# Ninety-six semaphore increments on SP behind each broadcast of lanes, in the layer 1 visits of a graph network

## What is computed

```
h = (x @ W).reshape(n, 4, 64)
h_l = (a_l * h).sum(-1);  h_r = (a_r * h).sum(-1)
e = h_l[row] + h_r[col];  e = where(e > 0, e, 0.2 * e)
ex = exp(e - segment_max(e, row)[row])
att = ex / (segment_sum(ex, row)[row] + 1e-16)
out = segment_sum(att[:, :, None] * h[col], row)
```

## Time and profile before

| | us |
|---|---|
| median of 3 runs | 4150.6 |
| lowest and highest of them | 4141.25, 4151.45 |
| the profiled execution | 4167.99 |
| its span, from the first to the last instruction | 4166.3 |
| the first and the last broadcast of lanes start at | 2048.0, 3372.1 |

### The profile page before, as it was taken

One profiled execution on the slowest core, in us unless ns is written; L12 is line 12 of the kernel. 1 busy time (PEld: TensorE's weight loads), 2 busy tenths in 40 slices (PEclk: granted clock), 3 DMA queues, 4 the chain that ended last, 5 costly groups with the idle time before them and its releaser, 6 DMA issues. The chain is left out here.

```text
span 4166.3 us, 48622 instructions
## 1 busy us (share of the span) xinstructions
PE 2771.2 (67%) x12850; PEld 2189.0 (53%) x12850; DVE 2489.0 (60%) x5847; ACT 1566.9 (38%) x5077; POOL 2220.9 (53%) x2162
## 2 busy tenths in 40 slices
PE   5466776567677754824666676666667665699983
PEld 4233344355555543713555465555555545599972
DVE  5345998677777786434545555555555567544438
ACT  6663000067787831113422232233233223333334
POOL 0366777766666602555256666666666641265530
PEclk9678888788898965967867767677776675799985
DMA  5232333323333313632234444444444464122234
GB/s 146 86 88 83 89 87 89 88 85 90 90 93 91 95 57 91 152 76 71 78 89 114 109 114 113 109 115 109 113 113 112 111 112 150 62 72 70 71 96 143
DMA packets 220767, 408.50 MB, mean 98 GB/s; under 512 B 51598, under 2 KB 134545, under 8 KB 220371
## 3 DMA queue, kind: packets, MB, share of 16 engines
q0 software_dynamic: 102192, 279.12, 25.2%
q1 hardware_dynamic: 118308, 126.27, 10.2%
HBM read 342.96 MB, written 62.28 MB: 97 GB/s over the span
## 5 line engine op out<-in xcount | busy, mean ns | idle before, releaser
L534 POOL DMA_INDIRECT arena<-h_table,arena x1712 | 1751.6, 1023 | 1016.0 <-issue 482.5
L548 DVE TENSOR_TENSOR arena<-arena,ps 128x260 f32 (+1 forms) x1712 | 719.6, 420 | 905.0 <-remote 407.0
L2199 PE MATMUL ps<-arena 128*128 128x260 f32 x1760 | 667.1, 538 | 415.9 <-DVE arena L548 282.6
L2199 PEld LDWEIGHTS ps<-arena 128*128 128x128 f32 x1760 | 441.5, 268 | 591.3 <-issue 457.0
L1216 PE MATMUL ps<-arena 128*128 128x256 f32 x1664 | 556.7, 451 | 252.5 <-DVE arena L548 133.1
L1216 PEld LDWEIGHTS ps<-arena 128*128 128x128 f32 x1664 | 328.1, 222 | 410.2 <-issue 238.2
L717 ACT ACTIVATE arena<-arena 128x112 f16<-128x112 f16 x1568 | 446.5, 375 | 88.1 <-DVE arena L983 77.6
L2066 ACT ACTIVATE ps<-arena 128x32 f32<-128x32 f32 x110 | 22.1, 201 | 953.8 <-DVE arena L2122 784.6
L884 DVE TENSOR_SCALAR arena<-arena 128x128 f32<-128x128 f32 x832 | 290.4, 350 | 0.4
L2181 PEld LDWEIGHTS ps<-arena 128*128 128x128 f32 x1760 | 273.2, 236 | 16.6 <-issue 4.5
L2132 DVE TENSOR_TENSOR arena<-arena,ps 128x1024 f32<-128x1024 f32 x220 | 267.2, 1215 | 0.0
(11 more groups left out here) (520 smaller groups left out, 4289.0 us busy)
## 6 DMA issues: line engine op xcount, KB each, us to landing
arena<-visit_lanes SPq DMA_DIRECT2D x110, 256.0 KB
arena<-h_table,arena POOLq DMA_INDIRECT x1712
arena<-in_L_ffn_w SPq DMA_DIRECT2D x32, 512.0 KB, 7.4
xn_table<-arena SPq DMA_DIRECT2D x14, 896.0 KB, 4.0
slot_out<-arena SPq DMA_DIRECT2D x21, 512.0 KB
arena<-y_rows SPq DMA_DIRECT2D x12, 896.0 KB, 9.5
h_table<-arena SPq DMA_DIRECT2D x7, 924.0 KB
h_table<-arena SPq DMA_DIRECT2D x7, 896.0 KB, 4.2
```

Of the source, the lines that this page charges most:

```text
L534: pool.indirect_dma_start(slot[:, 0:width], None, table, bass.IndirectOffsetOnAxis(ap=idx, axis=0)).then_inc(done, 16)
L548: dve.tensor_tensor(to, to, bank(b, width), ALU.add).then_inc(gnn_add, 1)
L2199: pe.matmul(bank(sum_bank(g * U + u), ACC_W), hot[:, g % 3, u, :], rows[r][:, u, 0:ACC_W], start=True, stop=True).then_inc(gnn_ps, 1)
```

## The change

One semaphore more, `beat`, and a constant, `BEATS` = 96. Behind each of the 110 broadcasts SP increments `beat` 96 times, each with an instruction of its own. Nothing waits for `beat`. There are 10,560 such instructions in the program; all else stays.

```
--- before.py
+++ after.py
@@ -2021,6 +2021,7 @@
         (rm_done, rm_ps, lc_done, hots_done, hott_done, look_ps, score_done, ex_done, msg_done, den_in) = (
             sem(n) for n in "rm_done rm_ps lc_done hots_done hott_done look_ps score_done ex_done msg_done den_in".split())
         lane_in = [sem(f"lane{b}_in") for b in range(2)]
+        beat, BEATS = sem("beat"), 96
         A = Steps(nc.scalar, sem("act_step"))
 
         def sum_bank(n):
@@ -2034,6 +2035,8 @@
                         sp.wait_ge(hott_done, g - 1)
                     sp.dma_start(lanes[g % 2], visit_lanes[g * U * P:(g + 1) * U * P].partition_broadcast(P)
                                  ).then_inc(lane_in[g % 2], 16)
+                    for _ in range(BEATS):
+                        sp.sem_inc(beat, 1)
 
             @block.gpsimd
             def _(pool):
```

## The result

| | before | after |
|---|---|---|
| median, us | 4145.9 (4 runs) | 4467.8 (4 runs, 4457.0 to 4483.9) |
| the profiled execution, us | 4168.0 | 4457.0 |
| its span, us | 4166.3 | 4455.2 |
| broadcasts of lanes, first to last | 2048.0 to 3372.1 | 2022.1 to 3667.0 |

The changed kernel is slower by 7.9%: the ratio is 1.0786, with an interval of 1.0753 to 1.082, or 322 us. The forecast was 4152 us, no change, with a range up to 4205. Both are missed.

What follows compares the result with a forecast made beforehand. The prediction saw layer 1's visits as a loop of hand-overs with no saturated engine. Steady state 0, start 1, end 0 and instruction stream 1 gave +2 us on 4150.6, about 4152 us; range 4125 to 4205 us.

Steps and rivals of the forecast that it cites:

- The price of an increment: On SP behind each broadcast: 0.05 us per increment, so a burst of 96 takes 4.8 us.
- near bound: Upper price from VectorE's 0.22 us pause for two instructions: 0.11 us per increment, 10.6 us a burst.
- far bound: Upper price from a whole DMA issue on SP: 0.32 us per increment, 30.7 us a burst.
- Rival A: At L2034's wait before each broadcast: SP becomes the bound above 0.121 us per increment; 4447 us at 0.15; chance 0.04.
- Slack: Steady state of layer 1's visits: SP needs 5.1 of 11.98 us per group, late broadcasts have cover; 0 us.
- The start: Block's first two broadcasts: second issued at 2053.1 us, its one-hot delayed up to 4.8 us; 1 us, ends 0 and 10.6.
- The instruction stream: Queue q14 loads 0.68 MB more in 83 packets, mostly beside gathers: 1 us, bounds 0 and 36 us.
- rival B: Code loading: all 36 us of packet time fall before a gather somebody waits for; 4187 us, chance 0.08.
- Rival C: In each group, SP's increments delay other engines' increments: 0.5 us a group, 53 us, 4204 us; chance 0.09.
- Rival D: At L548, late increments come sooner and remote waits shrink: at most 209 us, half gives 4046 us; chance 0.13.
- Rival E: At program build, increments nobody waits for are folded into one: 4151 us; chance 0.66 together with the forecast.
- The remote waits: VectorE's accumulations at L548 wait 349.5 us in 69 waits; read as not missing data for PE.

Runs made afterwards that it cites:

- after_b: The changed kernel again, against the kernel before, in a session where the kernel before took 3680.2 us: 3685.9 us, ratio 1.0016.
- mix16_b: Kernel before plus, per broadcast, 16 increments, 16 drains, 16 wait instructions on SP and 16 increments each on ScalarE, VectorE, TensorE: 4215.5 against 4142.9 us.
- mix16: Same added instructions as mix16_b, against the kernel before, in a session where that was fast: 3684.3 against 3685.5 us, one run each.

## Why the prediction was wrong, by its steps

**The price of an increment** is the step that failed. I took 0.05 us from SP's step between two instructions in quiet stretches. As a median it is right (0.058 us). But 96 in a row are priced by the mean, and in the condition of the two traces that was 0.152 us, three times as much, so that a burst took 14.6 us and not 4.8; my near bound, 0.11 us from VectorE's pause, was below it too; it was read at a single pair of additions. The far bound, 0.32 us, contained it, and I gave it no weight.

**Rival A** is what happened, with a chance of 0.04. Its point of decision was stated rightly, 0.121 us. At the measured 0.152 us its own formula gives 0.32 + 14.6 - 11.98 = 2.9 us, times 108 is 318 us, against 322 measured. That this comes so near is bookkeeping and no second proof: where SP hardly waits, a group lasts as long as SP's own instructions. Before the result nothing gave 0.152. Its signs came too: the wait of L2035 vanished and the distances grew.

**Slack.** "At least 10 us are free" in front of each use was right, and of no use: slack of that kind covers a late broadcast once, not an SP that needs more per group than the group lasts. The step I leaned on, that SP is back at its wait before the next one-hots end, held only in the free condition.

**The start.** SP and VectorE in order of time:

```profile
2036.12 0.34 SPq L2036 DMA_DIRECT2D arena<-visit_lanes  x1
...
2039.71 0.79 DVE L2109 TENSOR_SCALAR arena<-arena 128x1024 f32<-128x1024 bf16 x1 [11.78 <-DMA arena<-visit_lanes]
```

The second broadcast starts 14.0 us after the first (2022.09, 2036.12), not 5.1 us, since the first burst fell among gathers; the second one-hots waited 11.78 us. The wait that I named as cover, 23.45 us, is still there with 17.89 us, so part of the delay was absorbed. The forecast's upper end for the wait of the second one-hots was 10.6 us, a little too low.

**The instruction stream, rival B,** was right in its count (82 packets, forecast 83), and cost the kernel next to nothing: in the free condition, where its 10,560 instructions are loaded as well, the whole change costs 0.16%. The loading can be seen on SP, though. In after_b 82 steps, as many as the added packets, last over 0.3 us (0.37 us in the mean), one every 126 or 127 increments. That is 26 us of SP's time in all, hidden in its waits; as the prediction had it, only SP is stopped, for about the 0.3 us a group. **Rival C,** that increments hinder others, is neither shown nor refuted: 24 and 48 instructions on SP cost 0.7 and 0.5% with SP's waits left over, which would fit it, and its price of 53 us for 96 isn't contradicted. **Rival D** is gone: held up, no number of increments made anything faster. **Rival E** didn't happen: each of the 10,560 increments is in the trace.

**The remote waits** were the clue. I read the 9.83 us as a matter of PE's increments, asked whether SP might influence them, and did not ask the reverse: whether what delays PE's increments would delay SP's as well. That both come from one cause is an argument from the common step of 0.70 us and from their coming and going together. With a condition visible in which one engine's hand-overs take 10 us, a price for hand-overs on another engine had to come from inside that condition. The rows with PE's step of 0.70 us were there. With, say, one increment in seven at 0.7 us the mean is 0.15 us, beyond the point of decision.

A last part was beyond the profile: in the other condition the forecast holds (3685.9 against 3680.2 us). Nothing in one execution told that there were two.

**The rule of the page.** The rule of the Trainium skill in "TensorE: Matmul & The Clock Gate", section "The cost: per-tile semaphore tail", gave an estimate of 278 us for increments that serialize at 26.3 ns each. Its sum comes near the loss, its mechanism does not: in the free condition no step of SP is shorter than 45 ns; the shorter ones of the held-up condition (1,880 of 10,450 in after, down to 2 ns) come in its bunches and not at an even 26.3 ns; drains that write nothing are held up as well, and in the free condition 10,560 increments cost 6 us.

## What to carry to other kernels

An instruction that nobody waits for is free only while the queue that issues it has time left; write down the issuing engine's need per turn of the loop and the price at which it reaches the turn's length, and if the trace shows any stretch in which instructions are held up, take the mean price from there and not the median from a quiet one. Unexplained waits of one engine ("remote", "issue" at even steps) can be the mark of a condition that holds for other engines too, and a chance must be given that the added instructions live under it. Compare a kernel with its predecessor within one session only, and if the predecessor's own time jumps between sessions, measure the change in both. Count the trace's own records in both as well: where many are missing, the recording may be part of what is measured.

## What the runs showed of the hardware

- The same program took 4133 to 4187 us in four sessions and 3673 to 3690 us in the others, 12.5% apart, each steady within a session (to 0.5%). One chip showed both.
- In the slow condition, during gathers, instructions of several engines are held up, often by steps of about 0.70 us: SP's increments 0.227 us in the mean against 0.061 us, ScalarE's 0.166 against 0.070, VectorE's 0.126 against 0.095, PE's single matmuls and weight loads 0.70 us apart at the start of the block (but its own increments in mix16_b 0.161 against 0.155). GpSimd's gathers go on at 1.25 us.
- In that condition records of SP's increments come in bunches: steps down to 2 ns, 1,880 of 10,450 under 45 ns in after, none in after_b.
- In that condition PE's increments arrive together: before VectorE's addition at 2512.30 us the trace has four increments of `gnn_ps` at steps of 0.04 us, about 9 us after the end of the matmuls' records (2503.25 us).
- What holds the instructions up was not found. In that condition the traces hold 13,901 to 15,339 landing records instead of 38,681 to 39,114. All timed executions here were recorded with a trace, so that the recording itself may have a part in it; this was not tried.
- The instruction queue q14 brings 8 KB packets. In the free condition SP has one step of 0.37 us every 126 or 127 increments, 82 of them for 82 added packets.
- The steps of undisturbed sequencer instructions: SP 0.059 us per increment, 0.052 per drain; ScalarE 0.068, VectorE 0.093, TensorE 0.151 us per increment (medians of mix16).
